# Last stage of a decoder layer: transposes of h, gated z and rounded x move from TensorE to the DMA engines

## The chip, the cores and the metric

One core of a Trainium2 chip. The core has TensorE (PE, matrix products into the eight PSUM banks), VectorE (DVE), ScalarE (ACT), GpSimd (POOL), SyncE (SP, which here only issues DMAs) and 16 DMA engines. Each engine takes its instructions strictly in the order written and waits on semaphores. The metric is device time in microseconds (us).

## The reference, cut to what matters

x is 2 x 512 x 1024, so 1024 tokens, held as 8 tiles of 128 tokens.

```python
x = x + attention(layernorm(x))                       # 32 heads, 8 key/value heads
q1 = fake_quant(layernorm(x)); q2 = fake_quant(ctx)   # clip(round(v / s + zp), 0, 255), then (q - zp) * s
x = x + q1 @ q2                                       # 1024 x 1024 per batch
h = layernorm(x)
q = h @ Wq_w.T;  scores = q @ keys.T                  # router: 16 dims, 64 experts
gate = softmax(top 16 of scores), 0 elsewhere
z = (h @ A_w.T) * gate                                # 64 experts x rank 8 = 512 columns
x = x + (z @ B_w.T) * 2
```

## The kernel before

Attention takes most of the program. The change touches only the last stage, which comes after it and handles the last five lines of the reference for tiles t = 0 to 7 (TT = 8).

A float32 product is done as three float16 products: each operand is split into a high half (ACT, `split_hi`) and a low half (DVE, `split_lo`), and TensorE multiplies high by high, high by low and low by high (`split_product`, the matmuls of line L1581). TensorE contracts over partitions, so whatever stands on its left must lie with its contracted dimension on partitions: the rounded x, the normalised h and the gated z of a tile all have to be turned (128 x 128 blocks transposed) before use. Before the change TensorE turns all of them by a matmul against an identity, into PSUM, and ACT and DVE copy the result out:

- `turn_x` (L1815): 8 blocks of bf16 into bank 0; ACT copies them to `x_qt` (L1049).
- h3: 8 blocks of float32 (L1921) into banks 3 and 4; ACT and DVE write the two halves straight into `h3_t` (L748, L1106).
- `turn_z` (L1867): 4 blocks of float32 into bank 7; ACT and DVE write `z_t`.

Per tile the other products of TensorE are `x_product` (L1832, 16 matmuls: rounded x times the quantised context), the router (L1884, 16 small ones), z (24 of L1581), the scores (L1903) and `out_product` in two halves j = 0 and 1 (12 of L1581 each). DVE adds the product to x and takes its statistics (`x_half`, L1487 and L1490), finishes the reciprocal deviation with POOL's help (`bias3`, L1499), prepares the quantisation of the tile two ahead (`quantise_start`, `quantise_apply`, `quantise_end`: L1114, L1447, L1453, L1458), picks the 16 best experts (L1536 to L1544), gates z (L1550), and adds the output (`out_add`, L1479) and a correction term (`fold`, L1473). ACT normalises (h3, L1066), scales x for rounding (`scale_rows`, L1034), sums the rounded rows (`sum_rows`, L1039), and copies router and scores out of PSUM (L1059, L1073).

The order is written out by hand, as one loop per engine over i. In TensorE's iteration i stand: x_product(i), router and z of tile i-1, turn_x(i+1), scores of i-1, out_product(i-2, 0), turn of h3(i), out_product(i-2, 1), turn_z(i-1). So TensorE works on three tiles at once, and the engines wait for each other by counting semaphores. SP has nothing left in this stage but the eight stores of `out` (L600). The product of x and the output share banks 1 and 2; z has bank 5 alone.

The DMA transpose that the change uses is in the program already: in attention each unit's probabilities (128 x 1280, float16, high and low) are turned by two `dma_start_transpose` from SP (L530 and L533).

Of the kernel before, what the change touches and what calls it, by code (L numbers as in the profile page):

```python
# [6 lines left out]
ACT = mybir.ActivationFunctionType  # L7
F32 = mybir.dt.float32
F16 = mybir.dt.float16
# [74 lines left out]
def x_banks(t):  # L84

    return SECOND_X_BANK if t == 1 else X_BANK
# [105 lines left out]
def decoder_layer(nc, x, ctx_in, wq, wdown, wup, wo, a_w, b_w, router_w, keys, quant, ctx_whole, b_whole, kv_whole, out):  # L192
# [8 lines left out]
    with ctx:  # L201
# [76 lines left out]
        gated = q_tmp[:, 0, :]  # L278
        column_term = wq_in[:, :, :].rearrange("p a b -> p (a b)").rearrange("p (b n) -> p b n", b=BATCH)
# [104 lines left out]
        p_turned = [sem(f"p_turned{n}") for n in range(2)]  # L384
        pv_done = sem("pv_done")
# [30 lines left out]
        def _(sp):  # L416
# [329 lines left out]
        def _(act):  # L746
# [308 lines left out]
            for i in range(0, TT + STEPS_AHEAD):  # L1055
                if 0 <= i - 1 < TT:
                    t = i - 1
                    act.wait_ge(r_done, t + 1)
                    nc.scalar.activation(r_q[:, t % 2, :], ps[0:2 * ROUTER, SMALL_BANK, R_COL:R_COL + P], ACT.Copy,  # L1059
                                         scale=ROUTER_OUT).then_inc(r_copied, 1)  # L1060
                if 0 <= i < TT:
                    act.wait_ge(rstd3_done, i + 1)
                    if i >= 2:

                        act.wait_ge(h3_turned, 2 * (i - 1))
                    nc.scalar.activation(h3[i % 2], x_sb[:, i, :], ACT.Identity, bias=h3_bias[:, i:i + 1],  # L1066
                                         scale=rstd1[:, 2, 2 * TT + i:2 * TT + i + 1]).then_inc(h3_done, 1)
                if 1 <= i and i + 1 < TT:
                    copy_turned(i + 1)
                if 0 <= i - 1 < TT:  # L1070
                    t = i - 1
                    act.wait_ge(s_done, t + 1)
                    nc.scalar.activation(score[:, t % 2, :], ps[:, SMALL_BANK, S_COL:S_COL + EXPERTS], ACT.Copy)\  # L1073
                        .then_inc(s_copied, 1)
                    act.wait_ge(best_done, t + 1)
                    nc.scalar.activation(weight[:, t % 2, :], score[:, t % 2, :], ACT.Exp, bias=neg_best[:, t % 2:t % 2 + 1])\
                        .then_inc(weighted, 1)
                if 1 <= i and i + 1 < TT:
                    sum_rows(i + 1)
                if 1 <= i < TT - STEPS_AHEAD:  # L1080
                    scale_rows(i + STEPS_AHEAD)
                if 0 <= i < TT:
                    for j in range(2):
                        act.wait_ge(h3_turned, 2 * i + j + 1)
                        if j == 0 and i >= 2:

                            act.wait_ge(z_done, i - 1)
                        split_hi(h3_t[:, i % 2, 0, j * HALF:(j + 1) * HALF], ps[:, H_BANK[j], :], h3_hi, S_H)
                if i == 0:
                    scale_rows(STEPS_AHEAD)  # L1090
                if 0 <= i - 1 < TT:
                    t = i - 1
                    act.wait_ge(z_turned, t + 1)
                    split_hi(z_t[:, t % 2, 0, :], ps[:, ZT_BANK, :], zt_hi, 1.0)

        @block.vector
        def _(dve):
# [352 lines left out]
            def quantise_end(t):  # L1450
# [3 lines left out]
                if t >= 2:  # L1454

                    dve.wait_ge(x_turned, t - 1)
                    dve.wait_ge(row_summed, t - 1)
# [44 lines left out]
            def h3_split(t):  # L1502
                for j in range(2):
                    at = slice(j * HALF, (j + 1) * HALF)
                    dve.wait_ge(h3_hi, 2 * t + j + 1)
                    split_lo(h3_t[:, t % 2, 1, at], ps[:, H_BANK[j], :], h3_t[:, t % 2, 0, at], h3_lo, S_H)

            def z_split(t):
                dve.wait_ge(zt_hi, t + 1)
                split_lo(z_t[:, t % 2, 1, :], ps[:, ZT_BANK, :], z_t[:, t % 2, 0, :], zt_lo, 1.0)  # L1510
# [12 lines left out]
            for i in range(1, TT + STEPS_AHEAD):  # L1523
# [9 lines left out]
                if 0 <= i - 1 < TT:  # L1533
# [13 lines left out]
                    if t >= 1:  # L1547

                        dve.wait_ge(z_turned, t)
                    nc.vector.scalar_tensor_tensor(  # L1550
                        gated.rearrange("p (e r) -> p e r", r=RANK),
                        ps[:, Z_BANK, :].rearrange("p (e r) -> p e r", r=RANK), Z_OUT,
# [3 lines left out]
                    link(nc.vector.tensor_scalar(gate_scale[:, t:t + 1], gate_inv[:, t:t + 1], FFN_OUT, None, ALU.mult))  # L1556
                if 0 <= i - 2 < TT:
                    out_add(i - 2, 0)
                if i + STEPS_AHEAD < TT:
                    quantise_end(i + STEPS_AHEAD)  # L1560
                if i < TT:
                    h3_split(i)
                if i == TT:
                    z_split(i - 1)
                if 0 <= i - 2 < TT:
                    out_add(i - 2, 1)
                if 0 <= i - 1 < TT - 1:
                    z_split(i - 1)
                if 1 <= i and i + 1 < TT:
                    fold(i + 1)  # L1570

        @block.tensor
        def _(pe):
# [232 lines left out]
            def turn_x(t):  # L1806
# [5 lines left out]
                if t >= 2:  # L1812
                    pe.wait_ge(x_done, 2 * (t - 1))
# [159 lines left out]
```

## Time and profile before

| | us |
|---|---|
| median of 3 runs | 1117.89 (1117.43 to 1118.46) |
| the profiled execution | 1116.66 |
| its span | 1114.9 |
| PE busy | 1077.0 (97%) |
| DVE busy | 906.4 (81%) |
| ACT busy | 536.4 (48%) |
| POOL busy | 411.4 (37%) |
| mean granted TensorE clock | 0.994 |

The span is what the profile covers; the execution's own time is 1.76 us more. The chain that ended last is 87% PE. The last stage, from the first x_product at about 964.7 us to the end of the last matmul at about 1111 us, is some 13% of the span. In it the mean duration of a matmul says little, since matmuls overlap; the chain view shows what each group adds to the time.

### The profile page before, as it was taken

What the parts mean: (1) busy time and instruction counts of PE and PEld (TensorE: products, weight loads), DVE (VectorE), ACT (ScalarE), POOL (GpSimd) and SP (SyncE); (2) the same over time, 40 slices, a digit from 0 to 9 for tenths busy, and PEclk for the clock granted to TensorE, in tenths of its full rate; (3) what the DMA queues carried; (4) which work ended last, traced back from release to release, by engine and by line L of the source; (5) the groups of instructions that cost most, each with busy time, mean ns of one, the idle gap of its engine ahead of it and who ended that gap; (6) DMA issues with size and microseconds to landing.
All of it is one profiled execution on the core that took longest, in us unless ns stands there. A gap on an engine that the chain in (4) does not pass through costs nothing.

```text
span 1114.9 us, 19887 instructions
## 1 busy us (share of the span) xinstructions
PE 1077.0 (97%) x6368; PEld 581.8 (52%) x6368; DVE 906.4 (81%) x1868; ACT 536.4 (48%) x1094; POOL 411.4 (37%) x423
## 2 busy tenths in 40 slices
PE   4999998999999999999999999999999999899998
PEld 3976544555555555555555555555555554445554
DVE  6789578988787878788888878788878898888864
ACT  4656366555444545454445445444545462333421
POOL 2049755544343435344343544343535242000000
PEclk9999999999999999999999999999999999989999
DMA  8017246654454455455545554454554489000001
GB/s 313 1 59 254 77 88 142 156 120 119 125 129 113 99 137 139 110 124 123 124 103 122 136 129 96 120 134 113 115 138 117 111 188 271 12 1 39 20 39 57
DMA packets 200865, 128.66 MB, mean 115 GB/s; under 512 B 171376, under 2 KB 173552, under 8 KB 199920
## 3 DMA queue, kind: packets, MB, share of 16 engines
q1 hardware_dynamic: 200816, 128.03, 44.7%
q8 instruction: 28, 0.46, 0.2%
q14 instruction: 21, 0.17, 0.1%
HBM read 68.23 MB, written 17.83 MB: 77 GB/s over the span
## 4 chain that ended last, share of the span: by engine, by line
PE 87%; DVE 7%; ACT 3%; issue 1%; DMA 1%; POOL 1%; SPq 0%; DVEq 0%; ACTq 0%; POOLq 0%
PE ps L1581 82%; PE ps L1832 2%; ACT prob L975 1%; DVE prob L1315 1%; DVE h_b L1106 1%; DVE wo_sb L1106 1%; PE ps L1884 1%; DMA o_t<-in_wdown 1%; PE ps L1595 1%; DVE prob_t L1106 1%; PE ps L1921 0%; PE ps L1867 0%; DVE wq_sb L1106 0%; DVE stats L1114 0%; DVE o_t L1106 0%
## 5 line engine op out<-in xcount | busy, mean ns | idle before, releaser
L712 POOL TENSOR_SCALAR prob<-prob,row_inv 128x128 f32<-128x128 f32 (+3 forms) x256 | 203.4, 813 | 437.8 <-DVE row_inv L1286 437.8
L1581 PE MATMUL ps<-wo_sb,o_t 128*128 128x512 f16 x1536 | 351.3, 379 | 3.6 <-DVE x_sb L1297 3.6
L1581 PE MATMUL ps<-h_b,wq_sb 128*128 128x512 f16 x1524 | 344.0, 382 | 0.0
L975 ACT ACTIVATE prob<-prob,neg_max 128x128 f32<-128x128 f32 (+3 forms) x256 | 140.6, 550 | 220.8 <-DVE neg_max L1321 220.8
L1581 PEld LDWEIGHTS ps<-h_b,wq_sb 128*128 128x128 f16 x1524 | 149.2, 98 | 179.8 <-issue 4.7
L1581 PEld LDWEIGHTS ps<-wo_sb,o_t 128*128 128x128 f16 x1536 | 147.3, 98 | 171.7 <-DVE x_sb L1297 6.3
L1297 DVE SCALAR_TENSOR_TENSOR x_sb<-ps,x_sb 128x512 f32<-128x512 f32 x256 | 174.2, 686 | 53.1 <-PE ps L1581 52.3
L1581 PE MATMUL ps<-prob_t,v_sb 128*128 128x128 f16 (+2 forms) x960 | 115.6, 273 | 6.9 <-DMA prob_t<-prob_s 6.9
L1581 PE MATMUL ps<-k_t,q_t 128*128 128x512 f16 (+3 forms) x768 | 114.8, 299 | 0.5 <-DVE neg_max L1321 0.5
L1315 DVE CUSTOM_DVE_ANT_0 prob<-ps,mask 128x512 f32<-128x512 f32 (+3 forms) x256 | 110.3, 484 | 2.3 <-issue 1.6
L1581 PEld LDWEIGHTS ps<-prob_t,v_sb 128*128 128x128 f16 x960 | 83.1, 98 | 36.6 <-DMA prob_t<-prob_s 7.7
L748 ACT ACTIVATE q_t<-q_tmp 128x512 f16<-128x512 f32 x60 | 37.8, 630 | 131.8 <-DVE q_tmp L1273 131.8
L1273 DVE SCALAR_TENSOR_TENSOR q_tmp<-ps,q_tmp 128x512 f32<-128x512 f32 x105 | 72.1, 687 | 29.8 <-PE ps L1581 27.3
L1106 DVE SCALAR_TENSOR_TENSOR prob_s<-prob,prob_s 128x1280 f16<-128x1280 f32 x64 | 95.0, 1484 | 0.1
L748 ACT ACTIVATE prob_s<-prob 128x1280 f16<-128x1280 f32 x64 | 80.6, 1259 | 28.3 <-POOL prob L712 27.3
L1581 PEld LDWEIGHTS ps<-k_t,q_t 128*128 128x128 f16 x768 | 66.9, 98 | 51.6 <-issue 0.9
L1106 DVE SCALAR_TENSOR_TENSOR wq_sb<-wq_in,wq_sb 128x512 f16<-128x512 f32 x94 | 67.5, 733 | 0.5 <-ACT wq_sb L748 0.3
L1106 DVE SCALAR_TENSOR_TENSOR q_t<-q_tmp,q_t 128x512 f16<-128x512 f32 x60 | 62.1, 1055 | 0.7 <-ACT q_t L748 0.7
L742 POOL TENSOR_TENSOR rstd<-var_eps,minus_half 128x1 f32<-128x1 f32 x16 | 8.8, 548 | 144.5 <-DVE var_eps L1120 144.5
L1106 DVE SCALAR_TENSOR_TENSOR o_t<-ps,o_t 128x512 f16<-128x512 f32 x64 | 44.3, 692 | 20.1 <-ACT o_t L748 20.1
L748 ACT ACTIVATE wq_sb<-wq_in 128x512 f16<-128x512 f32 x94 | 56.6, 618 | 3.0 <-POOL wq_in L671 3.0
L975 ACT ACTIVATION_READ_ACCUMULATOR prob<-prob,neg_max 128x1 f32 x256 | 47.8, 187 | 0.0
(142 smaller groups left out, 1178.8 us busy)
## 6 DMA issues: line engine op xcount, KB each, us to landing
wq_in<-in_wq SPq DMA_DIRECT2D x64, 256.0 KB, 3.6
wo_in<-in_wo SPq DMA_DIRECT2D x32, 512.0 KB, 3.9
side_in<-in_ctx SPq DMA_DIRECT2D x16, 512.0 KB, 4.5
kv_parts<-wo_sb SPq DMA_DIRECT2D x7, 1024.0 KB, 5.2
x_sb<-in_x SPq DMA_DIRECT2D x8, 512.0 KB, 9.6
ctx_quantised<-side_out SPq DMA_DIRECT2D x16, 256.0 KB, 2.9
h_b<-ctx_quantised SPq DMA_DIRECT2D x2, 2048.0 KB, 10.8
out<-x_sb SPq DMA_DIRECT2D x8, 512.0 KB, 2.6
```

Source lines behind the costliest of these rows:

```text
L712: ins = nc.gpsimd.tensor_scalar(at, at, row_inv[:, u % 2, q:q + 1], S_P, ALU.mult, ALU.mult)
L742: nc.gpsimd.tensor_tensor(rstd0[:, k * TT + t:k * TT + t + 1], var_eps[:, k * TT + t:k * TT + t + 1], minus_half[:, :], ALU.pow).then_inc( ...
L748: nc.scalar.activation(dst, src, ACT.Copy, scale=scale).then_inc(signal, 1)
L975: ins = nc.scalar.activation(at, at, ACT.Exp, bias=neg_max[:, n % 2, q:q + 1], scale=SOFTMAX, accum_out=row_sum[:, n % 2, q:q + 1])
L1106: nc.vector.scalar_tensor_tensor(dst, src, scale, hi, ALU.mult, ALU.subtract).then_inc(signal, 1)
L1273: nc.vector.scalar_tensor_tensor(q_tmp[:, dst, :], ps[:, Q_BANK[product % 2], :], Q_OUT, q_tmp[:, src, :], ALU.mult, ALU.add).then_inc(com ...
L1297: nc.vector.scalar_tensor_tensor(at, ps[:, bank, :], WO_OUT, at, ALU.mult, ALU.add).then_inc(wo_read, 1)
L1315: ins = nc.vector.tensor_tensor_reduce(prob[:, u % 2, at:at + width], ps[:, at // HALF, at % HALF:at % HALF + width], mask[:, SEQ - width: ...
L1581: ins = nc.tensor.matmul(out_, lhs(i), rhs(j), start=start and n == 0, stop=stop and n == 3 * len(pairs) - 1)
L1595: ins = nc.tensor.transpose(ps[:, 2 * (t % 2) + j, k * P:(k + 1) * P], hn[:, t % 2, at:at + P], ident[:, :])
L1832: ins = nc.tensor.matmul(ps[:, x_banks(t)[j], :], x_qt[:, t % 2, k * P:(k + 1) * P], ctx_q[:, b, k, j * HALF:(j + 1) * HALF], start=k == 0 ...
L1884: ins = nc.tensor.matmul(ps[0:2 * ROUTER, SMALL_BANK, R_COL:R_COL + P], router_sb[:, k, :, :].rearrange("p a r -> p (a r)"), h3_t[:, t % 2 ...
```

## The change

Tiles in the middle no longer pass through TensorE to be turned. ACT and DVE split h3 and gated z where they lie in SBUF, into two staging tiles (`h3_s` over the weights' `wo_in`, `z_s` over `prob_s`), and SP turns each half with one DMA transpose into the places that TensorE read before. Rounded x is already bf16 in SBUF and is turned by one DMA. The exceptions stay with TensorE: x of tiles 0 and 1, h3 of tile 0, z of tile 7. TensorE loses the turns and keeps the products; the z product is cut into two runs of 12 matmuls with the scores between them. x products of tiles 2 to 7 get banks 3 and 4, and z alternates between banks 0 and 5. SP's order is, for each i: h3(i) high and low, z(i-1) high and low, x(i+2), store of tile i-2.

The diff without declarations of semaphores:

```diff
 def x_banks(t):
-    return SECOND_X_BANK if t == 1 else X_BANK
+    return (X_BANK, SECOND_X_BANK)[t] if t < 2 else H_BANK
+def z_bank(t):
+    return (TURN_BANK, Z_BANK)[t % 2]
+def h3_dmas(t):
+    return 32 * ((t + t % 2) // 2)
+def x_dmas(t):
+    return 16 * (t // 2)
+def z_dmas(t):
+    return 32 * (t // 2 + 1)
...
# SP
-            for t in range(TT):
-                sp.wait_ge(out_done, 2 * t + 2)
-                sp.dma_start(out[t], x_sb[:, t, :]).then_inc(stored, 16)
+            def turn_rounded(t):
+                sp.wait_ge(x_rounded, t + 1)
+                sp.wait_ge(x_done, 2 * (t - 1))
+                sp.dma_start_transpose(blocks(x_qt[:, t % 2, :]), x_q[:, t % 2, :]).then_inc(x_landed[t % 2], 16)
+            def turn_h3(t):
+                sp.wait_ge(h3_hi, t + 2)
+                sp.wait_ge(x_done, 2)
+                if t >= 2:
+                    sp.wait_ge(z_done, t - 1)
+                sp.dma_start_transpose(blocks(h3_t[:, t % 2, 0, :]), h3_s[:, t % 2, 0, :]).then_inc(h3_landed[t % 2], 16)
+                sp.wait_ge(h3_lo, t + 2)
+                sp.dma_start_transpose(blocks(h3_t[:, t % 2, 1, :]), h3_s[:, t % 2, 1, :]).then_inc(h3_landed[t % 2], 16)
+            def turn_gated(t):
+                sp.wait_ge(zt_hi, t + 1)
+                if t >= 2:
+                    sp.wait_ge(out_full, 2 * (t - 1))
+                sp.dma_start_transpose(blocks(z_t[:, t % 2, 0, :]), z_s[:, t % 2, 0, :]).then_inc(z_landed[t % 2], 16)
+                sp.wait_ge(zt_lo, t + 1)
+                sp.dma_start_transpose(blocks(z_t[:, t % 2, 1, :]), z_s[:, t % 2, 1, :]).then_inc(z_landed[t % 2], 16)
+            turn_rounded(2)
+            for i in range(1, TT + STEPS_AHEAD):
+                if i < TT:
+                    turn_h3(i)
+                if i - 1 < TT - 1:
+                    turn_gated(i - 1)
+                if i + STEPS_AHEAD < TT:
+                    turn_rounded(i + STEPS_AHEAD)
+                if i >= 2:
+                    t = i - 2
+                    sp.wait_ge(out_done, 2 * t + 2)
+                    sp.dma_start(out[t], x_sb[:, t, :]).then_inc(stored, 16)
...
# ACT: the new loop
+            h3_apply(0)
+            h3_high(0)
+            scale_rows(STEPS_AHEAD)
+            for i in range(1, TT + 1):
+                if i > 1:
+                    copy_small(i - 1)
+                if i < TT:
+                    h3_apply(i)
+                if i == 1:
+                    copy_small(0)
+                    sum_rows(STEPS_AHEAD)
+                t = i - 1
+                act.wait_ge(best_done, t + 1)
+                nc.scalar.activation(weight[:, t % 2, :], score[:, t % 2, :], ACT.Exp, bias=neg_best[:, t % 2:t % 2 + 1])\
+                    .then_inc(weighted, 1)
+                if i < TT:
+                    h3_high(i)
+                if i + STEPS_AHEAD < TT:
                     scale_rows(i + STEPS_AHEAD)
+                z_high(t)
+                if i + STEPS_AHEAD < TT:
+                    sum_rows(i + STEPS_AHEAD)
...
# DVE: splits from SBUF, and their place in the iteration
+                dve.wait_ge(h3_hi, t + 2)
+                split_lo(h3_s[:, t % 2, 1, :], h3[t % 2], h3_s[:, t % 2, 0, :], h3_lo, S_H)
...
+                if i < TT:
+                    h3_split(i)
+                if i + 1 < TT:
+                    fold(i + 1)
                 if 0 <= i - 2 < TT:
                     out_add(i - 2, 0)
+                if i <= TT:
+                    z_split(i - 1)
                 if i + STEPS_AHEAD < TT:
                     quantise_end(i + STEPS_AHEAD)
-                if i < TT:
-                    h3_split(i)
-                if i == TT:
-                    z_split(i - 1)
                 if 0 <= i - 2 < TT:
                     out_add(i - 2, 1)
-                if 0 <= i - 1 < TT - 1:
-                    z_split(i - 1)
-                if 1 <= i and i + 1 < TT:
-                    fold(i + 1)
...
# PE, in scores(t) and the loop
+                if t >= 1:
+                    pe.wait_ge(h3_landed[t % 2], h3_dmas(t))
+                    pe.wait_ge(s_copied, t)
...
+                z_part(t, range(0, KT // 2))
+                pe.wait_ge(r_copied, t + 1)
+                nc.tensor.matmul(ps[:, SMALL_BANK, S_COL:S_COL + EXPERTS], r_q[:, t % 2, :], keys_sb[:, :],
+                                 start=True, stop=True).then_inc(s_done, 1)
+                z_part(t, range(KT // 2, KT)).then_inc(z_done, 1)
+            turn_h3()
+            scores(0)
+            for i in range(2, TT + STEPS_AHEAD):
+                if i < TT:
+                    x_product(i)
+                if i - 1 < TT:
+                    scores(i - 1)
+                out_product(i - 2, 0)
+                if i == TT:
+                    turn_z()
+                out_product(i - 2, 1)
```

The order of instructions shows what moves. TensorE (PE), the start of a middle iteration of the kernel before: the turn of gated z, x_product, router, z, the turn of x, the scores.

```order
L1867 MATMUL ps<-ident,q_tmp 128x128 x4
L1832 MATMUL ps<-h_b,q_t 128x512 x16
L1884 MATMUL ps<-wq_sb,router_sb 32x128 x16
L1581 MATMUL ps<-h_b,wq_sb 128x512 x24
L1815 MATMUL ps<-ident_b,prob_t 128x128 x8
L1903 MATMUL ps<-keys_sb,mask 128x64
```

The same place now; the first row is the end of the output product that stands before x_product.

```order
L1672 MATMUL ps<-h_b,q_t 128x512
L1924 MATMUL ps<-h_b,q_t 128x512 x16
L1995 MATMUL ps<-wq_sb,router_sb 32x128 x16
L1672 MATMUL ps<-h_b,wq_sb 128x512 x12
L2007 MATMUL ps<-keys_sb,mask 128x64
L1672 MATMUL ps<-h_b,wq_sb 128x512 x12
```

Both turns are gone, and the scores stand in the middle of z. (The turn of h3, L1921 x8 between the two output halves, is gone in the same way.)

ACT, one middle iteration of the kernel before, with the semaphores each row waits for: router copy, h3, copy of turned x, scores copy, exponent, row sums, scaling of x, high halves of h3 and of z.

```order
L1059 ACTIVATE mask<-ps 32x128 [waits r_done]
L1066 ACTIVATE v_sb<-x_sb,h_bias,rstd 128x1024 [waits h3_turned,rstd3_done]
L1049 ACTIVATE q_t<-ps 128x1024 [waits x_turned]
L1073 ACTIVATE q_tmp<-ps 128x64 [waits s_done]
L1076 ACTIVATE q_tmp<-q_tmp,neg_best 128x64 [waits best_done]
L1039 ACTIVATE side_out,row_term<-prob_t,shift_scaled 128x1024 [waits x_rounded]
L1034 ACTIVATE prob<-x_sb,x_bias,x_scale 128x1024 [waits ln2_done]
L748 ACTIVATE wq_sb<-ps 128x512 [waits z_done,h3_turned]
L748 ACTIVATE wq_sb<-ps 128x512 [waits h3_turned]
L748 ACTIVATE q_t<-ps 128x512 [waits z_turned]
```

The same iteration now.

```order
L1116 ACTIVATE mask<-ps 32x128 [waits r_done]
L1119 ACTIVATE q_tmp<-ps 128x64 [waits s_done]
L1130 ACTIVATE v_sb<-x_sb,h_bias,rstd 128x1024 [waits h3_lo,h3_hi,rstd3_done]
L1168 ACTIVATE q_tmp<-q_tmp,neg_best 128x64 [waits best_done]
L807 ACTIVATE wo_in<-v_sb 128x1024 [waits h3_landed1,h3_done]
L1093 ACTIVATE prob<-x_sb,x_bias,x_scale 128x1024 [waits x_rounded,ln2_done]
L807 ACTIVATE prob_s<-q_tmp 128x512 [waits z_landed0,z_gated]
L1098 ACTIVATE side_out,row_term<-prob_t,shift_scaled 128x1024 [waits x_rounded]
```

The copy of turned x is gone, the scores are copied ahead of h3, and both high halves are made from SBUF, before h3 and z are turned.

## Rows read from the trace of the kernel before

**Rows 1.** The page, section 1: busy time of each engine.

```profile
PE 1077.0 (97%) x6368; PEld 581.8 (52%) x6368; DVE 906.4 (81%) x1868; ACT 536.4 (48%) x1094; POOL 411.4 (37%) x423
```

**Rows 2.** Chain that ended last, one tile's period; start us, us, what.

```profile
1008.18 3.45 PE ps L1832 x16
1011.64 1.00 PE ps L1884 x16
1012.64 5.29 PE ps L1581 x24
1017.92 0.45 PE ps L1815 x8
1018.37 0.36 PE ps L1903 x2
1018.73 2.70 PE ps L1581 x12
1021.42 0.87 PE ps L1921 x8
1022.30 2.59 PE ps L1581 x12
1024.89 0.44 PE ps L1867 x4
```

**Rows 3.** Timeline of DVE in that period; start, duration, instruction, [idle before].

```profile
1010.77 0.75 DVE L1487 SCALAR_TENSOR_TENSOR x_sb<-ps,both_scales,x_sb 128x512 f32<-128x512 f32 x1
...
1017.26 0.21 DVE L1447 SCALAR_TENSOR_TENSOR x_bias<-mean_var,x_scale,quant_sb 128x1 f32<-128x1 f32 x1
1019.58 0.23 DVE L1536 MAX8 best<-q_tmp 128x8 f32<-128x64 f32 x1 [2.11 <-ACT q_tmp L1073]
...
1021.07 0.69 DVE L1550 SCALAR_TENSOR_TENSOR q_tmp<-ps,q_tmp 128x512 f32<-128x512 f32 x1
...
1022.06 0.75 DVE L1479 SCALAR_TENSOR_TENSOR x_sb<-ps,gate_scale,x_sb 128x512 f32<-128x512 f32 x1
...
1027.91 0.75 DVE L1487 SCALAR_TENSOR_TENSOR x_sb<-ps,both_scales,x_sb 128x512 f32<-128x512 f32 x1
```

**Rows 4.** Line L530, its 64 DMA transposes: issue ns and landing, minimum/median/maximum.

```profile
L530 SPq DMA_TRANSPOSE prob_t<-prob_s x64: 1260/1350/2311, 146.9 to 928.7; - x64
...
DMA to landing us min/median/max: 3.3/3.4/6.7
```

**Rows 5.** The page, section 5: the splits of 1280 columns in SBUF.

```profile
L1106 DVE SCALAR_TENSOR_TENSOR prob_s<-prob,prob_s 128x1280 f16<-128x1280 f32 x64 | 95.0, 1484 | 0.1
L748 ACT ACTIVATE prob_s<-prob 128x1280 f16<-128x1280 f32 x64 | 80.6, 1259 | 28.3 <-POOL prob L712 27.3
```

**Rows 6.** Timeline of the stage's start, tiles 0 to 2, all engines.

```profile
977.41 7.39 PE L1581 MATMUL ps<-h_b,wq_sb 128*128 128x512 f16 x24
...
982.10 1.22 ACT L1066 ACTIVATE v_sb<-x_sb,h_bias,rstd 128x1024 f32<-128x1024 f32 x1
982.80 0.69 DVE L1458 TENSOR_SCALAR prob_t<-prob 128x1024 bf16<-128x1024 f32 x1
...
988.31 0.69 DVE L1550 SCALAR_TENSOR_TENSOR q_tmp<-ps,q_tmp 128x512 f32<-128x512 f32 x1
...
994.43 1.07 PE L1884 MATMUL ps<-wq_sb,router_sb 128*32 128x128 f16 x16
```

**Rows 7.** Windows at the start: busy time of each engine, PEclk, DMA share, GB/s.

```profile
972.00:975.60 3.60, 1.10 (x9) 0.86 (x9) 3.53 (x6) 1.95 (x3) 0.00 (x0) 0.88 0.01 2
...
978.00:981.60 3.60, 3.60 (x10) 1.21 (x8) 2.50 (x13) 0.80 (x1) 0.55 (x1) 0.50 0.00 0
...
986.60:989.00 2.40, 0.04 (x1) 0.00 (x0) 2.22 (x13) 1.74 (x4) 0.00 (x0) 0.88 0.00 0
989.00:992.00 3.00, 2.95 (x10) 1.65 (x11) 2.21 (x6) 2.32 (x4) 0.00 (x0) 0.53 0.00 0
```

**Rows 8.** Groups by form after 1000 us: the turn of h3, one of two buffers.

```profile
L1921 PE MATMUL ps<-ident,v_sb 128*128 128x128 f32 x24 | 3.1, 272 | 0.0
```

More of the change, by code:

```diff
@@ L384, in decoder_layer @@
         p_turned = [sem(f"p_turned{n}") for n in range(2)]
+        h3_landed = [sem(f"h3_landed{n}") for n in range(2)]
+        x_landed = [sem(f"x_landed{n}") for n in range(2)]
+        z_landed = [sem(f"z_landed{n}") for n in range(2)]
         pv_done = sem("pv_done")
@@ L597, in _, with blocks @@
             load_b_part(1)
-            for t in range(TT):
-                sp.wait_ge(out_done, 2 * t + 2)
-                sp.dma_start(out[t], x_sb[:, t, :]).then_inc(stored, 16)
+            def blocks(row):
+                return row.rearrange("p (k n) -> p k n", n=P)
+            def turn_rounded(t):
[29 more added lines that the diff above has]
+                    sp.dma_start(out[t], x_sb[:, t, :]).then_inc(stored, 16)
             sp.wait_ge(stored, 16 * TT)
@@ L1853, in out_product @@
             def out_product(t, j):
-                if t >= TT - 2:
+                if t == 0:
+                    pe.wait_ge(x_added, 2)
+                    for part in range(2):
+                        pe.wait_ge(b_loaded[part], 16)
+                if t >= 1:
                     pe.wait_ge(out_done, 2 * (t - 1) + j + 1)
+                if t < TT - 1:
+                    pe.wait_ge(z_landed[t % 2], z_dmas(t))
+                else:
+                    pe.wait_ge(zt_lo, TT)
                 split_product(ps[:, X_BANK[j], :],
@@ L1860, in out_product, with turn_h3, turn_z @@
                               ).then_inc(out_full, 1)
-            def turn_z(t):
-                pe.wait_ge(z_gated, t + 1)
-                if t >= 1:
-                    pe.wait_ge(zt_lo, t)
+            def turn_h3():
+                pe.wait_ge(h3_done, 1)
+                for j in range(2):
+                    for k in range(4):
+                        at = j * HALF + k * P
+                        ins = nc.tensor.transpose(ps[:, H_BANK[j], k * P:(k + 1) * P], h3[0][:, at:at + P], ident[:, :])
+                    ins.then_inc(h3_turned, 1)
+            def turn_z():
+                pe.wait_ge(z_gated, TT)
                 for k in range(BT):
@@ new lines, in z_part, with scores @@
+            def z_part(t, tiles):
+                return split_product(ps[:, z_bank(t), :],
+                                     [(lambda n, k=k: h3_t[:, t % 2, n, k * P:(k + 1) * P],
+                                       lambda m, k=k: a_sb[:, m, k // 2, (k % 2) * HALF:(k % 2 + 1) * HALF]) for k in tiles],
+                                     start=tiles[0] == 0, stop=tiles[-1] == KT - 1)
+            def scores(t):
+                if t == 0:
+                    pe.wait_ge(h3_lo, 2)
+                    pe.wait_ge(router_lo, 1)
+                    pe.wait_ge(wq_lo, 7 * (CYCLES - 1) + 11 + KT // 2)
+                if t >= 1:
+                    pe.wait_ge(h3_landed[t % 2], h3_dmas(t))
+                    pe.wait_ge(s_copied, t)
+                for n in range(2 * KT):
+                    k, part = n // 2, n % 2
+                    ins = nc.tensor.matmul(ps[0:2 * ROUTER, SMALL_BANK, R_COL:R_COL + P],
+                                           router_sb[:, k, :, :].rearrange("p a r -> p (a r)"),
+                                           h3_t[:, t % 2, part, k * P:(k + 1) * P],
+                                           start=n == 0, stop=n == 2 * KT - 1)
+                ins.then_inc(r_done, 1)
+                if t == 1:
+                    pe.wait_ge(x_added, 4)
+                if t >= 2:
+                    pe.wait_ge(z_gated, t - 1)
+                z_part(t, range(0, KT // 2))
[3 more added lines that the diff above has]
+                z_part(t, range(KT // 2, KT)).then_inc(z_done, 1)
```

167 lines of the change are left out of this document (61 added, 106 removed).

## Prediction

> **What bounds the kernel now.** I first read the busy times [rows 1]: PE 97%. A share over the whole span says nothing of the stage that changes, so next I took the chain of waits in the last stage. One tile's period [rows 2] is nine pieces, all PE, without a wait: 3.45 + 1.00 + 5.29 + 0.45 + 0.36 + 2.70 + 0.87 + 2.59 + 0.44 = 17.15 us. Three of them are turns: x 0.45, h3 0.87, z 0.44, together 1.76. Then DVE in the same period [rows 3]: it repeats at 1010.77 and 1027.91, 17.14 us, with one wait of 2.11 before the expert search. DVE thus needs 15.03 us per tile. PE is the bound, and DVE would be at 15.03; the reader should see how close the second engine stands.
>
> **The part that goes.** Without turns PE needs 17.15 - 1.76 = 15.39 per tile. I count the turns from the router of tile 1 on (994.43 [rows 6]), since before it PE still waits for others: x of tiles 3 to 7, 5 x 0.45 = 2.25; h3 of tiles 2 to 7, 6 x 0.87 = 5.22; z of tiles 1 to 6, 6 x 0.44 = 2.64. Sum 10.11 us, if PE stays without waits. The turn of z of tile 7 remains. Cutting z in two around the scores adds no instruction: 0.
>
> The duration of one turning matmul is 272 ns [rows 8], while the chain gives 0.87 / 8 = 0.109 us for each, because they overlap. The Trainium skill (TensorE: Matmul & The Clock Gate, Part 4: PE-mode transpose) prices one in a kernel at about 275 ns. The trace agrees on the duration, 272. Counted so, the 112 removed turns (40 of x, 48 of h3, 24 of z) would be an estimate of 30.8 us instead of 10.1; the chain decides, and the sum uses it.
>
> **What is added, in the steady state.** I set x_product(i) to start at 0 and PE to run without waits: x_product ends at 3.45, router 4.45, first half of z 7.10, scores 7.46, z 10.10, output halves 12.80 and 15.39. The next x_product ends, and h3(i) is due, at 18.84.
>
> DVE: x_half(i) starts about 0.15 after the first half product, at 1.9. From there to the end of x_bias it takes 1017.47 - 1010.77 = 6.70 [rows 3], so 8.6. The scores: before, scores ended at 18.73 and the search began at 19.58 (1018.73, 1019.58 [rows 2, 3]), 0.85 later; now 7.46 + 0.85 = 8.3, earlier than DVE arrives, so the 2.11 wait is gone. Gating comes 1.49 after the search (1021.07 - 1019.58), at 10.1; it must wait for z, 10.10 plus about 0.1, so 10.2. The low half of h3 starts 0.99 later (1022.06 - 1021.07), at 11.2. ACT has its high half ready: h3 takes 1.2 [rows 6], from about 8.0 to 9.2, then (with the exponent between) 1259 x 1024 / 1280 = 1.01 us [rows 5], at about 10.7. The low half takes 1484 x 0.8 = 1.19 [rows 5] and ends at 12.4.
>
> Its DMA transpose: 1280 columns land 3.4 us after issue, slowest 6.7, and SP is busy 1.35 for each [rows 4]. No row shows 1024 or 512 columns in this stage; the ends are 3.3 and 6.7, and I take 3.4, the median of 64 in a phase with far more DMA traffic. h3 lands at 12.5 + 3.4 = 15.9, due 18.84: 2.9 us hidden. DVE splits z of tile i-1 and rounds x of tile i+2 behind that and before its next x_half, at about 17.2, so even the last of them lands by 17.2 + 3.4 = 20.6; z is needed at 15.39 + 10.10 = 25.5, x by x_product(i+2) at 30.8. The store of tile i-2 comes behind them in SP's queue, and the next h3 high half only at 10.7 + 15.39 = 26.1, so SP delays nobody. SP issues 5 x 1.35 = 6.8 us of transposes per tile at most, under 15.39.
>
> DVE's period: 15.03 (it splits as many columns as before, from SBUF in place of PSUM), plus the wait of about 0.1 for z: some 15.15, against PE's 15.39. So PE still bounds, by 0.25 us: 0 in the sum. If this cover is gone each period costs what DVE exceeds.
>
> ACT loses the copy of turned x and has time left; only its order matters, below.
>
> **The start.** ACT now copies the router of tile 0 behind h3(1), which runs 982.10 to 983.32 [rows 6], so the scores of tile 0 wait until about 983.7, where the first half of z is done near 982 (half of the 7.39 from 977.41, a little more since the clock was low at first). The scores and the second half, 0.36 + 12 matmuls at z's 5.29 / 24 = 0.22 [rows 2], end near 986.7 instead of 984.8. Rounded x of tile 2 is ready at 983.49, lands at 987; x_product(2) runs to 990.4. h3(1) is the late one: gating at 988.31 [rows 6] plus 0.99 gives 989.3, low half to 990.5, landed at 994.0. So the router of tile 1 starts at 994.0 instead of 994.43: gain 0.45. This can be 1 us worse if PE's wait at 982 brings the clock down and z ends later.
>
> Here PE is idle from 990.4 to 994.0. The rows show what such gaps do: after 2.4 us idle (986.6 to 989.0) the granted clock was 0.53 over the next 3.0 us, that is mostly at 1.2 GHz; after 3.6 us with PE busy for only 1.10 (972.0 to 975.6) it was 0.50 up to 981.6, 6.0 us on [rows 7]. The first costs (1 - 0.53) x 3.0 = 1.4 us, the second 0.50 x 6.0 = 3.0. I take 2.2, the middle, because a gap of 3.6 us lies near both: -2.2.
>
> **The end.** For tile 7 no x_product(8) stands between, so h3(7) is due at 15.39 but lands at 15.9: -0.5. Behind it the order is as before.
>
> Sum: 10.1 + 0.45 - 2.2 - 0.5 = 7.85 us. The profiled execution took 1116.66 (span 1114.9, 1.76 around it), which gives 1108.8; the median is 1.23 above it, so 1117.89 - 7.85 = 1110.0.
>
> **Rivals.**
> A, DVE becomes the bound. For: only 0.25 us of room, so any wait in DVE's loop that I overlooked counts. Against: the one long wait that it has now goes. With 15.7 per tile over six periods: 6 x 0.3 = 1.8 less gain, plus 1 at the start: 1117.9 - 5.0 = 1112.9.
> B, the start and the clock cost nothing: h3(1) lands earlier because 1024 columns land faster than 1280. Then 10.1 + 0.5 and no wait at tile 7: 1107.3.
> C, slower than before: DMA transposes land late. Landing L costs L - 3.4 at tile 1, the same at tile 7, and, beyond the 2.9 hidden, L - 6.3 in each of five periods. With L = 6.7, the slowest of 64, 3.3 + 3.3 + 2.0 = 8.6: 1118.7, no change. Slower begins at L of about 7; at 7.5, 4.1 + 4.1 + 6.0 = 14.2, so 1124.2. For: five transposes per tile, two of h3 close together. Against: median 3.4, and the DMA engines are nearly idle here, 0.00 to 0.01 [rows 7].
>
> The Trainium skill (VectorE: DVE Perf Modes, The three transpose paths and Rules for kernel authors) speaks for C: 1309 ns for a 128 x 128 block by DMA against 390 by TensorE, and TensorE where PSUM will do. If blocks came one after another, 8 x 1.309 would be an estimate of 10.5 us to land, well on C's side. The trace doesn't agree: ten blocks land in 3.4.
>
> D, the change doesn't do what it says, because PE was only filling time and the loop hangs on another chain: 17.1 per tile as before. DVE's 15.03 and the unbroken PE chain speak against it. It would stay at 1117.9.
>
> **How the numbers follow.** Forecast (1108.5 to 1111.5) 0.55; A 0.18; B 0.12; C slow 0.05, C at about no change 0.04; D 0.06. About 0.2%, 2.2 us, is what a measurement of this kernel can tell from no change. Faster: 0.55 + 0.18 + 0.12 = 0.85; same 0.04 + 0.06 = 0.10; slower 0.05. The range runs from B to past A: low 1106.5 (B and a little), high 1113.5 (DVE 0.3 over, clock 3.0, start 1 late).
>
> **What would show it.** In the profile after: PE periods of 15.4 in the chain, with turns only for tile 0 (h3) and tile 7 (z); DVE's wait before the search gone, a short one before gating; transposes landing in about 3.4; PE idle some 3.6 us before the router of tile 1 with a granted clock near 0.5 behind it; a gap of about 0.5 before the router of tile 7. DVE periods over 15.5 or PE waits for DVE in the middle mean A; router rows that wait for the DMA in every tile mean C.

## The result, and the profile after

The changed kernel takes 1110.64 us (median of 4 runs, 1110.08 to 1111.37); the kernel before, run beside it, 1117.66 (4 runs, 1117.07 to 1118.46). The ratio is 0.9933, interval 0.9921 to 0.9944: faster by 0.67%, or 7.0 us. The forecast was 1110.0, within 1106.5 to 1113.5.

The page of the changed kernel, section 1, answers to [rows 1]: busy us, share of the span, instructions.

```profile
PE 1064.9 (96%) x6229; PEld 568.7 (51%) x6236; DVE 905.2 (82%) x1861; ACT 530.3 (48%) x1081; POOL 411.6 (37%) x423
```

PE has 12.1 us less work and DVE as much as before. (These 12.1 us are busy time, in which overlapping instructions count in part; the chain below decides.) That the share of PE fell by a point only says again that one stage is small in a whole span.

The chain that ended last in the changed kernel, one tile's period, answers to [rows 2]: start us, us, what.

```profile
1024.90 3.40 PE ps L1924 x15
1028.30 1.00 PE ps L1995 x16
1029.30 2.70 PE ps L1672 x12
1032.00 0.36 PE ps L2007 x2
1032.36 7.88 PE ps L1672 x36
1040.23 0.05 issue
1040.29 1.89 PE ps L1924 x8
```

The nine pieces are now five: product of x, router, first half of z, scores, and one unbroken piece of 36 matmuls (second half of z and both output halves). No turn and no wait stands between them. The period is 1040.29 - 1024.90 = 15.39 us, to the digit the sum of the prediction; the others are 15.38 or 15.39. (The product of x has 16 matmuls; where a row says 15, the record of its first one is missing from the trace. Distances that start at such a product are therefore taken below from its end.)

Timeline of DVE in the changed kernel, a later period, answers to [rows 3]: start, duration, instruction, in brackets the idle time before it.

```profile
1042.07 0.75 DVE L1572 SCALAR_TENSOR_TENSOR x_sb<-ps,both_scales,x_sb 128x512 f32<-128x512 f32 x1 [0.26 <-PE ps L1924]
...
1043.79 0.75 DVE L1572 SCALAR_TENSOR_TENSOR x_sb<-ps,both_scales,x_sb 128x512 f32<-128x512 f32 x1 [0.24 <-PE ps L1924]
...
1049.03 0.22 DVE L1628 MAX8 best<-q_tmp 128x8 f32<-128x64 f32 x1
...
1050.53 0.69 DVE L1643 SCALAR_TENSOR_TENSOR q_tmp<-ps,q_tmp 128x512 f32<-128x512 f32 x1
...
1051.51 1.22 DVE L1188 SCALAR_TENSOR_TENSOR wo_in<-v_sb,wo_in 128x1024 f16<-128x1024 f32 x1
...
1057.45 0.75 DVE L1572 SCALAR_TENSOR_TENSOR x_sb<-ps,both_scales,x_sb 128x512 f32<-128x512 f32 x1 [0.26 <-PE ps L1924]
...
1065.91 0.69 DVE L1643 SCALAR_TENSOR_TENSOR q_tmp<-ps,q_tmp 128x512 f32<-128x512 f32 x1 [0.83 <-DVE q_tmp L1636]
```

The wait of 2.11 us before the expert search (L1628) is gone. Two short ones are left, both for PE's product of x, 0.50 together, so DVE needs at most 15.38 - 0.50 = 14.88 us per tile. Before the gating (L1643) no wait is shown here: DVE arrives just as z is done. The wait for z that was foreseen there is seen where DVE has less to do, 0.83 us at 1004.38, 1065.91 and 1081.30; at the last two no tile is left to quantise. (The view puts it down to DVE's own L1636, which was done; the semaphore that came last is that of z.)

SP's own queue in the same stretch: its DMA transposes and the time to issue each, then their landing by the page (median us), in the order h3, z, x.

```profile
1050.80 1.24 SPq L636 DMA_TRANSPOSE wq_sb<-wo_in  x1
1052.77 1.23 SPq L638 DMA_TRANSPOSE wq_sb<-wo_in  x1
...
wq_sb<-wo_in SPq DMA_TRANSPOSE x14, 3.2
q_t<-prob_s SPq DMA_TRANSPOSE x14, 2.5
q_t<-prob_t SPq DMA_TRANSPOSE x6, 3.1
```

The low half of h3(5) is issued at 1052.77 and, with the median of 3.2, lands at 1055.97; the router of tile 5 begins at 1059.00. So the transfer has 3.0 us to spare, where 2.9 were foreseen. These halves answer to [rows 4]: 1024 columns land in 3.1 to 3.2 and 512 in 2.5, against 3.4 for 1280.

The chain at the start of the stage, with the first wait of PE, answers to [rows 6].

```profile
989.30 0.69 DVE q_tmp L1643
...
990.29 1.24 DVE wo_in L1188
...
991.54 3.23 DMA wq_sb<-wo_in
...
994.81 1.89 PE ps L1995 x16
996.70 4.53 PE ps L1672 x12
```

Windows there answer to [rows 7]: stretch, its length, busy us of PE, PEld, DVE, ACT, POOL, then PEclk, DMA share, GB/s.

```profile
991.20:994.80 3.60, 0.01 (x1) 0.00 (x0) 3.57 (x6) 0.12 (x2) 0.00 (x0) 0.83 0.81 156
994.80:998.00 3.20, 3.19 (x20) 2.17 (x21) 3.06 (x7) 1.39 (x3) 0.08 (x1) 0.50 0.96 87
998.00:1001.20 3.20, 3.20 (x11) 1.04 (x9) 2.89 (x14) 0.00 (x0) 1.02 (x2) 0.63 0.20 42
```

PE has its product of x of tile 2 done at 991.21 and stands still for 3.60 us for h3(1). Behind that the granted clock is 0.50 (all at 1.2 GHz) for 3.2 us and 0.63 for the next 3.2. The router takes 1.89 instead of the 1.07 that it takes behind a wait at full clock (tile 7, below), and 12 matmuls of z 4.53 instead of 2.70: 0.82 + 1.83 = 2.65 us lost.

The end, in the same chain: tile 7.

```profile
1078.51 1.97 PE ps L1672 x9
1080.48 0.82 issue
1081.30 0.69 DVE q_tmp L1643
...
1083.53 3.27 DMA wq_sb<-wo_in
...
1086.84 1.07 PE ps L1995 x16
```

x_product(7) ends at 1071.05 + 3.40 = 1074.45, and the router of tile 7 starts 12.39 after that. With h3 of all tiles early (below), where PE waits for nothing here, it is 11.86: 0.53 lost.

**The balance.** The profiled execution of the changed kernel reached the stage 1.0 us later than that of before, in work that the change does not touch: DVE's first addition of the stage starts at 967.49 against 966.50. The last matmul ends at 1104.46 against 1111.05. So the stage gained 7.6 us where the spans differ by 6.6 (1114.9 - 1108.3).

| Term | predicted | measured |
|---|---|---|
| turns gone, 5 x 0.45 + 6 x 0.87 + 6 x 0.44 | 10.11 | 10.1, by periods of 15.38 for 17.14 |
| router of tile 1 earlier in the stage | 0.45 | 0.61 |
| low clock behind the gap | -2.2 | -2.65 |
| h3 of tile 7 late | -0.5 | -0.53 |
| sum | 7.85 | 7.5 by the terms, 7.6 as a whole |

### The profile page after: what moved, and what is told of

Same layout as the page of the kernel before. It is cut to its first block, busy times and chain, and to the rows that moved or that the text cites. A ratio compares the mean times of both kernels' runs of the same rounds, so it can differ in the third digit from the quotient of the medians.

```text
span 1108.3 us, 19648 instructions
## 1 busy us (share of the span) xinstructions
PE 1064.9 (96%) x6229; PEld 568.7 (51%) x6236; DVE 905.2 (82%) x1861; ACT 530.3 (48%) x1081; POOL 411.6 (37%) x423
## 4 chain that ended last, share of the span: by engine, by line
PE 85%; DVE 8%; ACT 3%; issue 2%; DMA 1%; POOL 1%; SPq 0%; DVEq 0%; ACTq 0%; POOLq 0%
PE ps L1672 81%; PE ps L1924 2%; ACT prob L1034 1%; DVE wo_sb L1188 1%; DVE h_b L1188 1%; DVE prob L1397 1%; PE ps L1995 1%; DMA wq_sb<-wo_in 1%; DVE prob_t L1188 1%; DMA o_t<-in_wdown 1%; PE ps L1686 0%; ACT prob L890 0%; DVE stats L1196 0%; ACT wo_sb L807 0%; DVE wq_sb L1188 0%
## 5 line engine op out<-in xcount | busy, mean ns | idle before, releaser
L807 ACT ACTIVATE prob_s<-prob 128x1280 f16<-128x1280 f32 x64 | 80.6, 1259 | 28.0 <-POOL prob L771 27.3
```

The costliest lines, as they stand in the source:

```text
L807: nc.scalar.activation(dst, src, ACT.Copy, scale=scale).then_inc(signal, 1)
```

## The experiments

"Period" is the distance of the starts of two products of x in the profiled execution, "stage" the time from DVE's first addition of the stage (tile 0) to the end of the last matmul: 144.55 us before, 136.97 in the changed kernel. Ratios are to the kernel before on the same chip; its median beside the first four rows was 1117.69, beside the last three 1118.34, beside the others 1118.07. All variants start from the changed kernel.

| Variant | median us | ratio, interval | period | stage |
|---|---|---|---|---|
| changed kernel again | 1110.37 | 0.9934, 0.9913 to 0.9954 | 15.38 | 134.28 |
| gap filled | 1106.51 | 0.9907, 0.9889 to 0.9925 | 15.38 | 134.21 |
| h3 of tile 1 early | 1105.36 | 0.9888, 0.9871 to 0.9906 | 15.38 | 132.03 |
| h3 of all tiles early | 1103.94 | 0.9879, 0.9862 to 0.9896 | 15.38 | 131.19 |
| z turned by PE | 1109.85 | 0.9928, 0.9915 to 0.9941 | 15.82 | 136.92 |
| x turned by PE | 1109.02 | 0.9915, 0.9902 to 0.9928 | 15.83 | 136.31 |
| banks shared | 1108.09 | 0.9913, 0.99 to 0.9926 | 15.46 | 136.26 |
| DVE + 1.22 | 1108.04 | 0.9915, 0.9903 to 0.9928 | 15.38 | 134.32 |
| DVE + 2.44 | 1113.27 | 0.9951, 0.9931 to 0.997 | to 16.89 | 140.33 |
| one transpose more | 1113.35 | 0.9957, 0.9939 to 0.9975 | 15.38 | 138.36 |
| two transposes more | 1128.03 | 1.0077, 1.005 to 1.0105 | 16.6 | 156.47 |

**The changed kernel again.** No edit.

> The changed kernel once more, as the common measure on this chip. Every theory: ratio to the kernel before 0.993 to 0.994, 1110.6 us.

Measured: 1110.37, but over 1105.93 to 1112.2: two executions near 1106, one of 1109.06, three near 1112. The profiled one took 1106.02; it is called the second profile from here on. The windows of its gap and of what follows show most of the difference; columns as above.

```profile
989.80:993.40 3.60, 0.04 (x1) 0.00 (x0) 3.57 (x6) 0.13 (x2) 0.00 (x0) 1.00 0.81 158
993.40:997.00 3.60, 3.59 (x28) 1.99 (x28) 3.46 (x8) 1.39 (x3) 0.47 (x1) 1.00 0.72 96
```

The gap is the same, 3.57 us before the router of tile 1, and the clock stays at 1.00. From this router to the start of x_product(3) it took 12.06 us; in the first profile 14.71. So the low clock costs 2.65 us in one execution and nothing in another, with the same instructions. The same transposes are in flight here, and the durations are those of full clock, so contention with them is not what stretched the router and z in the first profile. In the second profile the clock was low earlier instead, over the first half of z of tile 0: it took 4.84 us (3.48 in the first profile, 2.76 at full clock). There the scores wait for ACT anyway, so it costs nothing. Of the 4.06 us between the two profiled executions 2.69 lie in the stage and 1.37 ahead of it; over all twelve profiles of the changed kernel and its variants the stage begins at 965.41 to 968.06. A median hides effects of 1 or 2 us under this; the undo experiments are therefore read by their periods, and their stages held against the second profile's.

**Gap filled.** 15 matmuls that nobody reads, into bank 7, between x_product(2) and the scores of tile 1:

```diff
+                if i == 2:
+                    pe.wait_ge(x_added, 4)
+                    for n in range(15):
+                        nc.tensor.matmul(ps[:, ZT_BANK, :], ones[:, :], ctx_sum[:, 0, 0:HALF], start=True, stop=True)
```

> Only addition: 15 matmuls of 128x512 (3.24 us at 0.216 each) into the unused bank 7, in the 3.6 us in which TensorE waits before the router of tile 1; they compute nothing that is used. Theory (the gap itself costs nothing more than the landing of h3(1), but the low clock behind it costs 0.89 at the router and 1.88 at the first half of z): both come down to 1.00 and 2.70, the time falls by 2.8 us against the changed kernel, to about 1107.9. Rival (the slow stretch is contention with the five transposes that land then, DMA share 0.96): no change, 1110.6, and the durations stay.

Measured: 1106.51. The router of tile 1 comes as late as before (27.27 us after the stage's start, 27.32 in the changed kernel), the clock is 1.00 and the stage takes 134.21, as in the second profile.

```profile
991.70:995.30 3.60, 3.32 (x16) 1.30 (x14) 3.56 (x6) 0.12 (x2) 0.00 (x0) 1.00 0.82 160
995.30:998.50 3.20, 3.17 (x27) 1.89 (x28) 3.06 (x7) 1.40 (x3) 0.03 (x1) 1.00 0.67 96
```

PE was busy for 3.32 of 3.60 us with work that nobody uses, and the stage is 2.76 shorter than in the first profile, with h3 as late: the loss belongs to the clock and not to h3's lateness. That filling the gap is what kept the clock up is not shown by this profile, since the second profile kept it without a filling. The medians differ by 3.9 with wide overlap (1105.88 to 1109.79 against 1105.93 to 1112.2). What speaks for the idling is the twelve profiles together: by the idle time of PE straight before the router of tile 1, the clock was low behind it in five of the seven with 2.19 us or more (3.60, 3.58, 3.58, 7.73, 2.19), full in the two others (3.57, and 3.62 in DVE + 1.22), and full in all five with 1.53 or less, two of them without any gap.

**h3 of tile 1 early.** ACT makes its high half ahead of the row sums of tile 2, and DVE the low half ahead of the expert search of tile 0:

```diff
# ACT, DVE
                 if i == 1:
                     copy_small(0)
+                    h3_high(1)
                     sum_rows(STEPS_AHEAD)
...
+                if i == 1:
+                    h3_split(1)
...
-                if i < TT:
+                if 1 < i < TT:
                     h3_split(i)
```

> ACT and DVE split h3 of tile 1 before the row sums and the expert search of tile 0; everything else stays. Theory (the wait at the start is DVE's order, the landing only 3.2 us of it): h3(1) lands about 990.7, before x_product(2) ends at 991.2, so the gap of 3.6 us and the 2.8 us of low clock both go; h3(2) then is late by about 1.0. Sum 3.6 + 2.8 - 1.0 = 5.4: 1105.2. Rival (the landing is what holds it, whatever the order): below 1 us of gain.

Measured: 1105.36. The router of tile 1 starts at 991.32, 23.73 after the stage's start instead of 27.32; one period then takes 15.74, since the chain behind it is DVE's. Stage 132.03: 2.2 less than with the filled gap, and no gap to lower the clock. The rest of the 3.6 is lost on the way: the scores of tile 1 now wait 0.94 for ACT, whose copy of the router stands behind the row sums, and the long period takes 0.36.

**h3 of all tiles early.** The same, and DVE splits h3 ahead of the gating in every tile:

```diff
+                    if 1 < i < TT:
+                        h3_split(i)
                     dve.wait_ge(z_done, t + 1)
...
-                if 1 < i < TT:
-                    h3_split(i)
```

> As the one with h3(1) early, and in addition DVE makes the low half of h3 before it waits for z and gates, in every tile. Theory: h3(2) and h3(7) come about 1.1 us earlier, so neither is waited for: 3.6 + 2.8 + 0.4 = 6.8 us under the changed kernel, 1103.8. Rival (gating comes later and is itself waited for): as the one with h3(1) early or worse, 1105 to 1107.

Measured: 1103.94 (1103.33 to 1104.46), the fastest of all, 1.2% under the kernel before. The chain at tile 7, last piece before the router:

```profile
1072.54 7.88 PE ps L1675 x36
1080.42 1.00 PE ps L1998 x16
```

PE goes into the router of tile 7 without a wait, which was the term of 0.5. From the scores of tile 1 on, which wait 0.84 for ACT, PE never stands still. Stage 131.19: 3.1 less than in the second profile, 5.8 less than in the first.

**z turned by PE again**, the other two by DMA:

```diff
-                if i - 1 < TT - 1:
-                    turn_gated(i - 1)
...
-                if i == TT:
-                    turn_z()
+                if i <= TT:
+                    turn_z(i - 1)
```

> Gated z of every tile is turned by TensorE again (bank 7, between the two output halves); h3 and x stay with the DMA. Theory (TensorE is the bound in every period, so a turn costs its whole place in the chain): 6 x 0.44 = 2.64 us more than the changed kernel, 1113.3. Rival (DVE or a chain through it has become the bound): under 1 us, 1110.6 to 1111.6.

Measured: 1109.85. The chain shows the turn (L1974) back in its place, at its price:

```profile
1045.57 5.29 PE ps L1670 x24
1050.85 0.44 PE ps L1974 x4
1051.29 2.59 PE ps L1670 x12
```

Periods 15.82 for 15.38: 0.44 each, as the term says. The total missed the expectation by 3.5 us and was no slower than the changed kernel's. PE at the start of the stage in this kernel tells why.

```profile
983.02 0.43 PE L2006 MATMUL ps<-keys_sb,mask 32*128 32x64 f32 x2 [4.02 <-ACT mask L1114]
983.39 4.45 PE L1670 MATMUL ps<-h_b,wq_sb 128*128 128x512 f16 x12
987.66 3.63 PE L1922 MATMUL ps<-h_b,q_t 128*128 128x512 bf16 x16
991.13 0.60 PE L1974 MATMUL ps<-ident,q_tmp 128*128 128x128 f32 x4
993.26 1.07 PE L1994 MATMUL ps<-wq_sb,router_sb 128*32 128x128 f16 x16 [1.53 <-DMA wq_sb<-wo_in]
```

Here the first half of z of tile 0 ran at full clock, the wait for the scores was 4.02 us, and the clock was low behind it: the second half of z took 4.45 us for 2.76. That delays the product of x of tile 2 by 1.4 us and nothing more, since h3(1) is later still; it only shortens the gap, to 1.53. Behind that the clock is full. So the low clock fell where it is covered, and this run is to be held against the second profile: 136.92 - 134.28 = 2.64, where 6 x 0.44 = 2.64 was due. Only the four full periods, 1.76 of it, are the turn alone; the turn of z(1) also waits 0.51 for DVE, and the wait of tile 7 hides its turn, so that the sum agrees to the digit is partly luck.

**x turned by PE again**, into bank 7, copied by ACT:

```diff
-                if i + STEPS_AHEAD < TT:
-                    turn_rounded(i + STEPS_AHEAD)
...
                 if i - 1 < TT:
                     scores(i - 1)
+                if i + 1 < TT:
+                    turn_x(i + 1)
```

> Rounded x of every tile is turned by TensorE again and copied by ACT (bank 7); h3 and z stay with the DMA. Theory: 5 x 0.45 = 2.25 us more than the changed kernel, 1112.9; up to 1.4 less than that if the later x_product(2) shortens the gap before the router of tile 1 and with it the low clock. Rival (the bound is elsewhere): 1110.6.

Measured: 1109.02, periods 15.83: 0.45 each, the term of x. Stage 136.31 against the second profile's 134.28: 2.03 more, where 5 x 0.45 = 2.25 was due; the wait of tile 7 is 0.23 shorter here. The expected 1112.9 is missed as with z, and the total is no higher than the changed kernel's; the expectation named the reason but allowed 1.4 for it: the product of x of tile 2 waited for ACT's copy and ran later, PE idled 0.68 us before the router of tile 1, and no low clock followed it.

**Banks shared.** The products of x go back into banks 1 and 2 beside the output:

```diff
-    return (X_BANK, SECOND_X_BANK)[t] if t < 2 else H_BANK
+    return SECOND_X_BANK if t == 1 else X_BANK
...
+                        pe.wait_ge(out_done, 2 * (t - 3) + j + 1)
...
+                pe.wait_ge(x_added, 2 * min(t + 3, TT))
```

The last line makes the output of tile t wait in turn until DVE has emptied the banks of the product of x.

> x products of tiles 2 to 7 go back to banks 1 and 2, which they share with the output; the rest stays as in the changed kernel. Theory (DVE empties each bank before it is wanted, by 0.2 us): 1110.6, at most 1 us more. Rival (banks of their own are part of the gain): each period waits for DVE, 5 x 0.5 = 2.5 us or more, 1113.

Measured: 1108.09, periods 15.46 (+0.07). (The total falls with where the low clock lay, as with z: over the second half of z of tile 0, and in part behind the router of tile 1.) PE's weight loads wait for the addition of the output (L1564), as the waits of this kernel from tile 2 on show (what waits for what: us in total, times, longest):

```profile
PEld ps L1924 <- DVE x_sb L1564: 1.6, 4, 0.4
```

Of each 0.4 us 0.07 reach the period. Over five tiles the banks of their own are worth 0.07 x 5 = 0.4 us.

**DVE + 1.22**: one addition of 128x1024 more in tiles 2 to 7, result unused:

```diff
+                    nc.vector.scalar_tensor_tensor(q_tmp[:, 2:4, :].rearrange("p a b -> p (a b)"), x_sb[:, i, :], 1.0,
+                                                   x_sb[:, i, :], ALU.mult, ALU.add)
```

> One extra DVE instruction of 128x1024 (1.28 us) per tile 2 to 7, behind the rounding; its result is not used. DVE then needs 14.9 + 1.28 = 16.2 per tile against TensorE's 15.39. Theory (h3 lands 3.0 us before it is due, so DVE may fall behind by 0.8 per tile over four tiles before anyone waits): at most 1 us more, 1110.6 to 1111.6. Rival (DVE's room of 0.25 to 0.5 us is the whole cover): 0.8 x 5 = 4 us more, 1114.6.

Measured: 1108.04 and periods of 15.38, unchanged. SP's queue, low halves of h3 of tiles 4, 5 and 7:

```profile
1034.42 1.23 SPq L638 DMA_TRANSPOSE wq_sb<-wo_in  x1
...
1050.23 1.23 SPq L638 DMA_TRANSPOSE wq_sb<-wo_in  x1
...
1078.81 1.24 SPq L638 DMA_TRANSPOSE wq_sb<-wo_in  x1
```

The first two are 15.81 us apart: DVE now needs 15.8 (14.6 without the 1.22, so even 14.88 holds some slack) and falls back 0.43 from one tile to the next. Held against the end of the tile's product of x, the low half is issued 2.18 later than in the changed kernel at tile 5, the most of any (11.26 for 9.08), and h3 has 3.0 us to spare. In the last two iterations DVE has no tile left to quantise and catches up: at tile 7, which has nothing to spare, the distance is 9.07 again. So the stage is as long as in the second profile, 134.32 for 134.28. The theory put down here, that h3's spare covers DVE's lag, holds; the prediction had counted every period of DVE over 15.39 as lost at once, and that was wrong.

PE stood idle before the router of tile 1 for as long as in the first profile, and the clock behind it was full:

```profile
992.75 1.07 PE L1998 MATMUL ps<-wq_sb,router_sb 128*32 128x128 f16 x16 [3.62 <-DMA wq_sb<-wo_in]
```

**DVE + 2.44**: the same twice.

> Two extra DVE instructions of 128x1024 per tile 2 to 7. With one of 1.22 us h3 fell back by 0.43 per tile while the periods of TensorE stayed at 15.38, so DVE needs 14.6 per tile by itself and 17.0 here. Theory (3.0 us of cover are used up after two tiles, then DVE sets the period): two periods of 15.4, then 17.0; some 4 to 5 us more than the changed kernel, 1114 to 1116. Rival (cover of another size): periods stay at 15.4 throughout, or are 17.0 from the first.

Measured: 1113.27. Periods 15.38, 15.39, 15.58, 16.89: first nothing, then the whole. PE waits 2 times for h3's transfer, 3.6 us in all (the router of tile 5, 1.43, and that of tile 7, 2.20, of which 0.4 was there before). DVE is 14.6 + 2.44 - 15.4 = 1.6 us too slow per tile. The low half of tile 4 is issued 3.13 later than in the changed kernel, and its router is held up by 0.2; that of tile 5 is 4.67 later and costs 1.5. So the cover ends near 3.0 us. The clock was low behind the gap here, so the stage is held against the first profile's: 140.33 - 136.97 = 3.4 longer, where 4 to 5 were expected.

**One transpose more**, of 1024 unused columns, issued ahead of the low half of h3:

```diff
                 sp.wait_ge(h3_lo, t + 2)
+                for n in range(1):
+                    if t > 1 or n > 0:
+                        sp.wait_ge(spare_landed, 16 * (1 * (t - 1) + n))
+                    sp.dma_start_transpose(blocks(spare_t), spare_s).then_inc(spare_landed, 16)
```

> One more DMA transpose of 1024 columns (its result is not used) in SP's queue ahead of the low half of h3, in every tile, so that h3 lands 1.25 us later. Theory (landing is hidden by 3.0 us in the middle, by nothing at tiles 1 and 7): periods of TensorE stay at 15.38, the router of tile 1 comes 1.3 later against x_product(2), tile 7 1.3 later: 2.6 us in sum. Rival (transposes share the DMA engines, so one more delays all and the periods grow): periods of 16 or more.

Measured: 1113.35, periods 15.38. The router of tile 7 starts 13.70 after the end of its product of x instead of 12.39 (+1.31), the router of tile 1 comes 1.4 later (28.73 after the stage's start for 27.32). The chain at tile 7:

```profile
1082.50 1.23 SPq L644
...
1083.78 3.31 DMA wq_sb<-wo_in
```

The price is SP's issue time, 1.23, and what lies between the rows (1083.78 - 1082.50 = 1.28), and a little slower landing. It is paid at both ends of the loop and nowhere in the middle. Against the second profile the stage is 4.1 longer: 1.4 + 1.3, and 1.3 of low clock behind the gap (16.77 from the router of tile 1 to the end of the next product of x, for 15.46).

**Two transposes more**, each waiting for the one before to land (the edit is against the variant with one):

```diff
-                for n in range(1):
+                for n in range(2):
```

> Two more DMA transposes of 1024 columns, one after the other has landed, ahead of the low half of h3 in every tile: 3.2 + 1.25 = 4.5 us later. Theory: beyond the 3.0 us of cover every period waits, first 1.5 us, and 4.5 at tiles 1 and 7; periods 15.4 + 1.5 if nothing else gives way, sum 5 x 1.5 + 2 x 4.5 = 16, about 1126. Rival (the cover is larger than I think): periods stay at 15.4, sum 9.

Measured: 1128.03, slower than the kernel before. The chain, in every tile now:

```profile
1023.98 1.24 DVE wo_in L1195
...
1025.23 3.17 DMA q_tmp<-ctx_sum
...
1028.41 1.23 SPq L644
...
1029.70 3.32 DMA wq_sb<-wo_in
...
1033.06 1.07 PE ps L2002 x16
```

h3 is issued 29.70 - 25.23 = 4.47 us later than it could be. Less the 3.0 to spare, 1.4 should reach the period; it grew by 1.2 (16.55 to 16.59, once 16.97). The start pays 4.16 of it. The router of tile 7 is 7.9 late (20.31 behind the end of its product of x for 12.39): 4.1 for its own h3, 2.2 because the router of tile 6 before it is held up too, and 1.7 of low clock behind that wait. Another 2.8 of low clock follow the router of tile 7 (1.89 and 4.66 for router and first half of z, for 1.07 and 2.70).

## Why the prediction was right

**PE bounds the stage, and the turns stood in its chain.** Right. Period 15.38 to 15.39 for 15.39, and putting z or x back costs 0.44 and 0.45 per tile. h3's 0.87 was not put back alone; it follows from the difference of the periods (17.15 - 15.38 - 0.89 = 0.88), which is arithmetic and no experiment. The duration of one turn, 272 ns, would have given a gain three times too large, so the chain was the right view to price from. (The 112 turns that the prediction calls the removed ones are those from the router of tile 1 on, which its sum counts; 132 went in all.)

**The transfers are hidden.** Right, with the size: 3.0 us to spare for 2.9 predicted. Three experiments show the spare by its limit: a lag of 2.2 at tile 5 and one of 1.3 in each tile are taken up, one of 3.1 costs 0.2, and one of 4.5 in each tile adds 1.2 to every period. Rival C is a real mechanism that stood 3 us off. Its prediction for a landing of 7.5 was 1124.2; two transposes more, 4.5 late, gave 1128.0, of which 2.8 are low clock in tile 7 that C had not counted.

**DVE would be just hidden, by 0.25 us.** The outcome was right, and the step on DVE was not. DVE needs 14.6 by the run with 1.22 more, and not 15.15, so the room is 0.8; how the difference splits over its instructions was not measured. And exceeding 15.39 costs nothing until the spare of h3 is used up. Rival A gave 1.8 us for 0.3 too much over six periods; 0.43 too much per tile cost nothing, since the lag only adds up to tile 5. It was given 0.18 and deserved less.

**The start.** The router of tile 1 comes 0.61 earlier for 0.45. The scores of tile 0 did wait for ACT, by 2.49 us, and where the clock fell behind this wait (z turned by PE, banks shared) it did not delay the router of tile 1, because h3(1) is later still.

**The clock.** -2.2 predicted as a middle of 1.4 and 3.0; the first profile shows -2.65. What the step missed is that it is no constant: 2.65 us or nothing behind the same gap. That the measured median came within 0.7 us of the forecast is partly luck: the first four runs, 1110.08 to 1111.37, all lie among the longer ones of the changed kernel. Rival B's gain, 10.6, is near the 144.55 - 134.28 = 10.3 of the stage in the second profile, but only for the half of its reason that names the clock: h3(1) did not land early enough to close the gap, which was 3.57 us there too, and tile 7 waited as before.

**Tile 7.** -0.53 for -0.5, and it goes when h3 is split before the gating.

## What to carry to other kernels

When a turn moves from the bounding engine to the DMA queues, price it by its share of that engine's chain, and price the transfer by when its result is due. The slack between landing and due time also absorbs the lag of the engine that feeds the transfer, so an engine that is a little too slow costs nothing in a short loop. Look for the cost at the loop's ends, where no other tile's work stands between: here splitting h3 sooner, without one instruction less, gave another 6.4 us by the medians (1110.4 to 1103.9); by the stages it is 3.1 where the clock was full behind the gap and 5.8 where it was low.

## What the runs showed of the hardware

- After the same 3.6 us of idle PE the granted clock fell to 0.50 (1.2 GHz) in one execution and stayed 1.00 in another, where it had been low for longer some 15 us earlier. In DVE + 1.22 it also stayed full after 3.62 us, without having been low for longer before (3.31 us for the first half of z of tile 0, 3.48 in the first profile). What decides where a low stretch falls was not found.
- A low stretch costs only where nothing later holds PE up anyway: with the second half of z of tile 0 at 4.45 us for 2.76 (z turned by PE, banks shared) the router of tile 1 still came 27.1 to 27.3 us after the stage's start.
- DMA transposes from SBUF to SBUF: SP issues one in 1.20 to 1.27 us at 512 and at 1024 columns, and now and then in 2.2 to 2.8; 1024 columns of two bytes land in 3.1 to 3.2 us, 512 in 2.5 (medians).
- Where the transposes of several tiles fall together, at the stage's start, the DMA engines show 0.81 and 0.96 busy, against 0.47 over a later period (1024.9 to 1040.3); h3 still landed in 3.23.
